# Ternary weight quantisation of the third feed-forward moved into the loop of the cross attention ahead of it

## The chip, the cores and the metric

The kernel runs on one core of one Trainium2 chip. The metric is the device time of one launch, in microseconds (us), as the median of several runs. One execution was also recorded by the hardware profiler; all rows below come from that execution.

## What is computed

The reference is a decoder of four layers on an input of 16 sequences of 128 tokens, width 256. Each layer adds an attention (or a recurrent mixer), a cross attention and a feed-forward to the residual stream `x`, each on the layer norm of `x`. The change touches two neighbours of the third layer, the cross attention and the feed-forward:

```python
def _L2_xattn_ref(q, kv, seg_id, W_kvc, W_dq, W_uq, W_qr, W_uk, W_kr, W_uv, W_o):
    kv_c = kv @ W_kvc; q_c = q @ W_dq            # latents of width 64 and 96
    # 16 heads of 128 (+ 64 rotary), scores, window mask, softmax, weighted values, @ W_o
...
def ternary_quant(w_fp32, g=64):
    w = w_fp32.astype(jnp.bfloat16)
    w_g = w.reshape(-1, g)
    scale = jnp.clip(jnp.mean(jnp.abs(w_g), axis=-1, keepdims=True), 1e-08, None)
    q = jnp.clip(jnp.round(w_g / scale), -1, 1)
    w_hat = (q * scale).reshape(w.shape)
    return w + jax.lax.stop_gradient(w_hat - w)
...
def _L2_ffn_ref(x, w_gate_up, w_proj):           # w_gate_up 2048 x 256, w_proj 256 x 1024
    gate, up = jnp.split(jnp.einsum('bsd,hd->bsh', x, ternary_quant(w_gate_up)), 2, axis=-1)
    hn = rms_norm(jax.nn.silu(gate) * up)
    return jnp.einsum('bsh,dh->bsd', hn, ternary_quant(w_proj))
...
x = x + _L2_xattn_ref(_layernorm(x), ctx_2048, itok, ...)
x = x + _L2_ffn_ref(_layernorm(x), L2_ffn_w_gate_up, L2_ffn_w_proj)
```

The quantised weights don't depend on `x`: they can be made at any time after the weights are loaded.

## The kernel before

The program is a row of twelve phases (attention, cross attention, feed-forward, four times), each written as one or two blocks in which every engine has its own instruction stream; streams meet only at semaphores, and all engines meet at the end of a block. The residual `x` stays on chip (128 partitions x 16 tiles of 256). A phase walks it in 4 groups (`GROUPS`) of 4 tiles (`TG`), 512 tokens at a time. Weights of a phase lie in one of two halves of an arena (`k.arena(n)`, tile `w` of the whole program, in the rows `all_w`); `after(sp)` is the call with which a phase lets SyncE (SP) clear the other half's semaphores and issue the loads of the next phase into the half that is free. `own` is the semaphore and count that say a phase's own weights have landed.

`phase_xattn2` (names `xattn_*` in the rows) is the third cross attention. A first block, "prep", makes products of weights: TensorE multiplies, ScalarE and VectorE copy and split them (L2792 to L2843). SP issues four small loads there (three of `l2x_qr`, one of `seg`), counted by the semaphore `small`, and the first piece of the context. ScalarE's rounding of the loaded `raw` (L2816) and VectorE's last splits (L2843) wait for `small`. The second block is a hardware loop of four passes (`Fori`), one for each group. A pass on VectorE: a mask (L2936 to L2942), the low part `ql` of the query latent (L2944), nine rotary products (L2957, L2958, L2950), then for `n` in 0 to 11 scores, maxima, normalisation, and four additions into `x` (`add`, L2988). The last, `add(3)`, waits for TensorE's last output projection (L3086); TensorE opens the next pass only after it (`step_open`). `Chain` is a helper that makes each VectorE instruction wait for the one before it. ScalarE begins a pass with `kL` (L2887). SP's stream in this block ends with `after(sp)`, behind the loads of the other context pieces.

`phase_ffn2` (names `ffn_*`) is the feed-forward; the common part is `gated_ffn`. Its first pass also prepares the weights in six chunks of 1024 columns: ScalarE casts a chunk to bf16 (L3177), VectorE's `encode` makes the 16 group scales and the codes (L3235 to L3240), GpSimd multiplies codes by scales (L3246), VectorE's `replace` forms `w + (w_hat - w)` (L3251, L3252), TensorE transposes the chunk (`turn`, L3201) and ScalarE copies it out of PSUM into `w1` or `w3` (`copy`, L3167, L3171). Chunk 0 comes ahead of the first matmul, chunks 1 to 3 ahead of the column blocks f = 2, 4, 6 of the first pass (there are 8, f = 0 to 7, each with 16 matmuls at L1179 every two), chunks 4 and 5 after them. TensorE waits for each copy before it goes on. Then come the output projection (L1188), the row sums for the RMS norm (L1196) and, in the other three groups, the same pass with no preparation.

Of the kernel before, what the change touches and what calls it, by code (L numbers as in the profile page):

```python
# [1029 lines left out]
def gated_ffn(k, w1, w2, w3, F, after, norm, parts, first, step, rms_eps=None):  # L1030
# [1680 lines left out]
def phase_xattn2(k, arena, own, after):  # L2711
# [155 lines left out]
    steps = Signal(k, "vector_steps", 5)  # L2867

    with nc.Block() as block:
        @block.sync  # L2870
        def _(sp):
# [4 lines left out]
            after(sp)  # L2876
# [52 lines left out]
        def _(dve):  # L2929
            chain = Chain(dve, steps)  # L2930
            dve.sem_inc(norm.step_open.sem, 1)
            with dve.Fori(0, GROUPS) as i:
# [57 lines left out]
                for n in range(U + 4):  # L2990
# [131 lines left out]
def phase_ffn2(k, arena, own, after):  # L3122
# [12 lines left out]
    w = k.sb("w", [P, CHUNKS, CW], BF16)  # L3135
    ratio = k.sb("ratio", [P, CW], BF16)
    code = k.sb("code", [P, 2, CW], BF16)
    scale = k.sb("scale", [P, CHUNKS, CG, 1], BF16)
    total = k.sb("total", [P, CHUNKS, CG, 1])
    inv = k.sb("inv_scale", [P, CHUNKS, CG, 1])  # L3140
    rounded = Signal(k, "rounded")
    coded = Signal(k, "coded")
    scaled = Signal(k, "codes_scaled")
    quantized = Signal(k, "quantized")
# [8 lines left out]
    def raw(c):  # L3153
        return up[:, :, c] if c < UPS else down[:, :, c - UPS]

    def rows(c):
        if c < UPS:
            return w[:, c].rearrange("p (b j n) -> p b j n", b=2, j=2)
        return w[:, c].rearrange("p (r n) -> p r n", r=KC)
# [29 lines left out]
    def turn(pe, c):  # L3189
        pe.wait_ge(*quantized(0, c + 1))  # L3190
        if c >= 2:
            pe.wait_ge(*copied(0, c - 1))
        r = rows(c)
        for h in range(KC):
            for b in range(2):
                for j in range(2):
                    if c < UPS:
                        src, at = r[:, b, j, h * P:(h + 1) * P], h * 2 * D + b * D + j * P
                    else:
                        src, at = r[:, h, (2 * b + j) * P:(2 * b + j + 1) * P], (2 * b + j) * D + h * P  # L3200
# [27 lines left out]
    def grouped(a):  # L3228
        return a.rearrange("p (g n) -> p g n", n=TGRP)

    def encode(dve, c):
        chain = chains.setdefault(0, Chain(dve, steps))
        wc = grouped(w[:, c])
        dve.wait_ge(*rounded(0, c + 1))
        chain(dve.tensor_reduce(total[:, c, :, 0], wc, AX.X, ALU.add, apply_absolute_value=True))  # L3235
        chain(dve.tensor_scalar(scale[:, c], total[:, c], 1.0 / TGRP, 1e-8, ALU.mult, ALU.max))
        chain(dve.reciprocal(inv[:, c], scale[:, c]))
        chain(dve.tensor_tensor(grouped(ratio[:, :]), wc, inv[:, c].broadcast_to([P, CG, TGRP]), ALU.mult))
        chain(dve.tensor_scalar(ratio[:, :], ratio[:, :], -1.0, 1.0, ALU.max, ALU.min))
        dve.tensor_scalar(code[:, c % 2], ratio[:, :], ROUND, ROUND, ALU.add, ALU.subtract).then_inc(coded.sem, 1)  # L3240
        dve.wait_ge(*coded(0, c + 1))

    def scale_codes(pool, c):
        qc = grouped(code[:, c % 2])
        pool.wait_ge(*coded(0, c + 1))
        pool.tensor_tensor(qc, qc, scale[:, c].broadcast_to([P, CG, TGRP]), ALU.mult).then_inc(scaled.sem, 1)  # L3246

    def replace(dve, c):
        chain = chains[0]
        dve.wait_ge(*scaled(0, c + 1))  # L3250
        chain(dve.tensor_tensor(code[:, c % 2], code[:, c % 2], w[:, c], ALU.subtract))  # L3251
# [1247 lines left out]
```

## Time and profile before

| | |
|---|---|
| median of 3 runs | 2396.2 us (2394.41 to 2402.05) |
| the profiled execution | 2391.62 us |
| its span, first to last instruction | 2389.8 us |
| TensorE busy over the span | 2103.3 us (88%) |
| VectorE / ScalarE / GpSimd busy | 66% / 52% / 13% |
| mean granted TensorE clock | 0.939 of full speed |

A busy share is an average over twelve unlike phases: it doesn't say what bounds one of them. "Idle before" an instruction is the time its engine had nothing to do just ahead of it, with what ended that time behind the arrow. Matmul ends are modelled, and a matmul's duration overlaps the next one's, so distances between starts are the better measure. PEclk is the share of TensorE's full clock (2.4 GHz) that was granted: 1.00 or 0.50, and means between them.

### The profile page before, as it was taken

To read this page: it belongs to the slowest core of one execution; us is meant where nothing else is said; L and a number is where in the kernel's file an instruction comes from. 1 tells how busy PE (TensorE), PEld (TensorE's weight loads), DVE (VectorE), ACT (ScalarE), POOL (GpSimd) and SP (SyncE) were. 2 spreads that over 40 slices of the span, in tenths; PEclk is the share of its full clock that TensorE was granted. 3 is DMA by queue.
4 is the path that set the end of the run, shared out by engine and by line. 5 is a ranking of instruction groups with operands and counts; after the bars stand their busy time and mean duration, and the time that the engine had idled before them with its cause. 6 is when DMAs were issued, how large, how long until landed. Compare 5 with 4: busy or idle time off the path is not lost. (4 is left out here: it accounts for less than half of the span.)

```text
span 2389.8 us, 46874 instructions
## 1 busy us (share of the span) xinstructions
PE 2103.3 (88%) x18948; PEld 1595.6 (67%) x18951; DVE 1576.4 (66%) x2957; ACT 1238.2 (52%) x2457; POOL 316.9 (13%) x315
## 2 busy tenths in 40 slices
PE   7979979899899898888889998958989879999996
PEld 5644437677655687566656666647756668999996
DVE  4443476667565897877858666877576676676663
ACT  3336714544466443555536446644468614666653
POOL 0010000011210000001000000011100114444342
PEclk9989989899999998999989999978989878999998
DMA  2020001100110002000010010010200025666673
GB/s 98 22 81 10 2 14 54 36 1 1 40 37 2 33 1 70 1 1 1 1 32 1 9 61 0 0 36 1 71 1 2 6 72 175 216 208 202 199 219 86
DMA packets 62649, 125.59 MB, mean 53 GB/s; under 512 B 16056, under 2 KB 45369, under 8 KB 62297
## 3 DMA queue, kind: packets, MB, share of 16 engines
q1 hardware_dynamic: 53626, 110.83, 13.8%
q0 software_dynamic: 8832, 12.06, 2.4%
q8 instruction: 138, 2.26, 0.4%
q14 instruction: 53, 0.43, 0.1%
HBM read 109.18 MB, written 15.80 MB: 52 GB/s over the span
## 5 line engine op out<-in xcount | busy, mean ns | idle before, releaser
L262 PE MATMUL ps<-ffn_xh,ffn_wh 128*128 128x256 f32 x644 | 184.0, 286 | 1.5 <-DVE ffn_xl L4283 1.5
L262 PE MATMUL ps<-ffn_xh,ffn_wl 128*128 128x256 f32 x644 | 182.3, 283 | 0.0
L262 PE MATMUL ps<-ffn_xl,ffn_wh 128*128 128x256 f32 x644 | 182.2, 283 | 0.0
L4278 DVE TENSOR_TENSOR ffn_wl<-ffn_fresh,ffn_wh 128x1792 fp32r<-128x1792 f32 x69 | 139.4, 2023 | 26.2 <-ACT ffn_wh L4158 21.1
L210 POOL TENSOR_TENSOR all_rstd<-all_mv,all_cst 128x4 f32<-128x4 f32 x41 | 9.6, 233 | 1031.8 <-DVE all_mv L193 1031.8
L1890 DVE SCALAR_TENSOR_TENSOR attn_xc<-attn_cx,all_w,attn_xc 128x512 f32<-128x512 f32 (+1 forms) x144 | 107.2, 749 | 48.0 <-ACT attn_xc L1741 44.4
L262 PEld LDWEIGHTS ps<-ffn_xh,ffn_wh 128*128 128x128 f32 x644 | 123.5, 192 | 1.7 <-DVE ffn_xl L4283 1.7
L4158 ACT ACTIVATE ffn_wh<-ffn_fresh 128x1792 fp32r<-128x1792 f32 x69 | 117.1, 1697 | 14.6 <-DMA ffn_fresh<-in_l3f_w 14.6
L262 PEld LDWEIGHTS ps<-ffn_xl,ffn_wh 128*128 128x128 f32 x644 | 123.4, 192 | 0.0
L262 PEld LDWEIGHTS ps<-ffn_xh,ffn_wl 128*128 128x128 f32 x644 | 123.4, 192 | 0.0
L2901 ACT ACTIVATE xattn_sc<-xattn_sc,xattn_mx 128x128 f32<-128x128 f32 x256 | 98.8, 391 | 17.7 <-DVE xattn_mx L2975 17.7
L4145 POOL DMA_INDIRECT x_acc<-ffn_y,ffn_row_i x46 | 79.2, 1721 | 215.0 <-ACT ffn_y L4186 212.0
L1920 DVE TENSOR_TENSOR attn_e<-attn_e,all_w 128x1024 f32<-128x1024 f32 (+1 forms) x80 | 87.2, 1124 | 16.4 <-ACT attn_e L1774 15.1
L262 PE MATMUL ps<-ffn_wh,ffn_hh 128*128 128x256 f32 x322 | 94.2, 293 | 3.9 <-issue 2.6
L1179 PE MATMUL ps<-ffn_xh,ffn_w 128*128 128x512 f32 x224 | 92.0, 411 | 6.2 <-ACT ffn_w L3167 4.5
L254 PE MATMUL ps<-all_xnT,all_w 128*128 128x512 f32 (+1 forms) x176 | 90.0, 643 | 4.1 <-ACT all_xnT L753 2.6
L262 PE MATMUL ps<-ffn_wl,ffn_hh 128*128 128x256 f32 x322 | 91.1, 283 | 0.0
L262 PE MATMUL ps<-ffn_wh,ffn_hl 128*128 128x256 f32 x322 | 91.0, 283 | 0.0
L1179 PE MATMUL ps<-ffn_xl,ffn_w 128*128 128x512 f32 x224 | 90.5, 404 | 0.0
L248 PE MATMUL ps<-all_cst 128*128 128x512 f32 x102 | 60.1, 743 | 29.6 <-ACT attn_zs L1761 10.2
L200 DVE TENSOR_SCALAR all_xn<-all_x,all_mv,all_rstd 128x256 f32<-128x256 f32 (+1 forms) x164 | 59.9, 430 | 37.5 <-POOL all_rstd L212 37.4
L4301 DVE TENSOR_TENSOR all_xnT<-ps,all_xn 128x512 f32<-128x512 f32 x92 | 57.2, 622 | 41.6 <-PE ps L262 38.7
(483 smaller groups left out, 6114.6 us busy)
## 6 DMA issues: line engine op xcount, KB each, us to landing
ffn_fresh<-in_l3f_w SPq DMA_DIRECT2D x69, 896.0 KB, 5.0
all_w<-in_ctxT SPq DMA_DIRECT2D x12, 512.0 KB, 6.2
all_w<-in_ctx SPq DMA_DIRECT2D x8, 512.0 KB, 6.5
all_x<-in_x_rows SPq DMA_DIRECT2D x4, 512.0 KB, 7.3
all_x<-x_seq SPq DMA_DIRECT2D x4, 512.0 KB, 5.4
all_w<-in_l2x_o SPq DMA_DIRECT2D x1, 2048.0 KB, 9.2
xattn_ctxT<-in_ctxT SPq DMA_DIRECT2D x4, 512.0 KB, 3.7
all_w<-in_l2f_up SPq DMA_DIRECT2D x1, 2048.0 KB, 9.1
```

The costliest lines, as they stand in the source:

```text
L200: dve.tensor_scalar(k.xn[:, t, :], k.x[:, i * TG + t, :], k.mv[:, t, 0:1], k.rstd[:, t, 0:1], ALU.subtract, ALU.mult).then_inc(self.xn_rea ...
L248: pe.matmul(k.psum[bank][:, :], k.c["ident"], k.cst[:, 0:512], start=True, stop=True)
L254: last = pe.matmul(out, w[:, c, n0:n1], k.xnT[:, c, a:b], start=start and c == 0, stop=stop and c == KC - 1)
L262: last = pe.matmul(out, a, b, start=start and n == 0, stop=stop and n == 2)
L1179: last = pe.matmul(out, w[:, c, f * P:(f + 1) * P], part[:, c, :], start=c == 0 and n == 0, stop=c == KC - 1 and n == 1)
L1890: ins = dve.scalar_tensor_tensor(out, cx[0:n, c % 2, :, j:j + P], tap, out, ALU.mult, ALU.add)
L1920: dve.tensor_tensor(e[:, d % SLOTS_E], e[:, d % SLOTS_E], gm[:, q % 2].unsqueeze(1).broadcast_to([P, HP, P]), ALU.mult).then_inc(m_ready.s ...
L2901: last = act.activation(s, s, ACT.Exp, bias=mx[:, n % nS, e, h:h + 1], scale=-1.0, accum_out=total[:, n % nS, e, h:h + 1])
L4145: pool.indirect_dma_start(acc[:, :], bass.IndirectOffsetOnAxis(ap=row_i[:, at:at + 1], axis=0), y[:, j % 2, v, :], None, compute_op=ALU.ad ...
L4158: act.activation(wh[:, j % 2, piece(q)], fresh[:, piece(q)], ACT.Copy).then_inc(high_ready.sem, 1)
L4278: dve.tensor_tensor(wl[:, j % 2, piece(q)], fresh[:, piece(q)], wh[:, j % 2, piece(q)].bitcast(F32), ALU.subtract).then_inc(low_ready.sem, 1)
L4301: dve.tensor_tensor(h[:, n % 2, 0:width], B[n % 2][:, 0:width], sa[:, n % 2, 0:width], ALU.mult).then_inc(h_ready.sem, 1)
```

## The change

- The loads of the feed-forward's weights (`after(sp)`) are issued at the head of SP's stream in the cross attention's prep block, ahead of its small loads, and no longer in the loop block.
- In each of the four passes of the cross attention ScalarE casts a quarter of the weights (1536 columns) to bf16 at the pass's head; VectorE makes the 24 group scales behind `ql`, and rounds, scales and forms the result behind `add(2)`, ahead of `add(3)`. The result is written as bf16 over the first half of the quarter's own bytes in the arena. A new semaphore pair, `tw_ready` and `tw_done`, orders the cast and the rounding; ScalarE also waits once for the loads (`k.next_own`).
- The multiplication by the scale is done by VectorE, no longer by GpSimd.
- The feed-forward's first pass has only the transposes and the copies left. The first transpose stands ahead of the layer norm's, and its copy ahead of the norm's copies. The chunks that are transposed are the same.

```diff
+    ternary = ternary_flat(k.arena(8)).rearrange("p (g n) -> p g n", g=GROUPS)
+    codes = ternary_codes(k.arena(8))
+    CW = ternary.shape[2]
+    CG = CW // TGRP
+    tw = k.sb("ternary_w", [P, CW], BF16)
+    ratio = k.sb("ternary_ratio", [P, CW], BF16)
+    group_scale = k.sb("ternary_scale", [P, CG, 1], BF16)
+    group_sum = k.sb("ternary_sum", [P, CG, 1])
+    group_inv = k.sb("ternary_inverse", [P, CG, 1])
+    tw_ready = Signal(k, "ternary_w_ready", 1)
+    tw_done = Signal(k, "ternary_w_done", 1)
...
             def _(sp):
+                after(sp)
                 qr = k.ins["l2x_qr"].rearrange("c (h r) -> c h r", h=MH)
...
                 sp.wait_ge(*ctx_used(i, 1))
                 sp.dma_start(ctxT[:, :, :], src[i + 1]).then_inc(ctx_loaded.sem, 16)
-            after(sp)
...
+            act.wait_ge(*k.next_own)
             with act.Fori(0, GROUPS) as i:
+                act.wait_ge(*tw_done(i, 1))
+                act.activation(tw[:, :], ternary[:, i, :], ACT.Copy).then_inc(tw_ready.sem, 1)
...
+            dve.sem_inc(tw_done.sem, 1)
...
+                def scale_ternary():
+                    dve.wait_ge(*tw_ready(i, 1))
+                    chain(dve.tensor_reduce(group_sum[:, :, 0], grouped(tw[:, :]), AX.X, ALU.add, apply_absolute_value=True))
+                    chain(dve.tensor_scalar(group_scale[:, :, :], group_sum[:, :, :], 1.0 / TGRP, 1e-8, ALU.mult, ALU.max))
+                    chain(dve.reciprocal(group_inv[:, :, :], group_scale[:, :, :]))
+
+                def round_ternary():
+                    wide = [P, CG, TGRP]
+                    chain(dve.tensor_tensor(grouped(ratio[:, :]), grouped(tw[:, :]), group_inv[:, :, :].broadcast_to(wide),
+                                            ALU.mult))
+                    chain(dve.tensor_scalar(ratio[:, :], ratio[:, :], -1.0, 1.0, ALU.max, ALU.min))
+                    chain(dve.tensor_scalar(ratio[:, :], ratio[:, :], ROUND, ROUND, ALU.add, ALU.subtract))
+                    chain(dve.tensor_tensor(grouped(ratio[:, :]), grouped(ratio[:, :]), group_scale[:, :, :].broadcast_to(wide),
+                                            ALU.mult))
+                    chain(dve.tensor_tensor(ratio[:, :], ratio[:, :], tw[:, :], ALU.subtract))
+                    dve.tensor_tensor(codes[:, i, 0:CW], tw[:, :], ratio[:, :], ALU.add).then_inc(tw_done.sem, 1)
+
+                scale_ternary()
...
                     if n >= 5 and n % W == 1:
+                        if n == U + 3:
+                            round_ternary()
                         add((n - 5) // W)
...
+def ternary_flat(arena):
+    return arena[:, 0:2 * TF // P * D + KC * TF]
+
+
+def ternary_codes(arena):
+    return ternary_flat(arena).bitcast(BF16).rearrange("p (g n) -> p g n", g=GROUPS)
...
     def scalar(act):
-        act.wait_ge(*own)
-        for c in range(CHUNKS):
-            act.activation(rows(c), raw(c), ACT.Copy).then_inc(rounded.sem, 1)
-            if c == 2:
-                norm.scalar(act, 0)
         copy(act, 0)
+        norm.scalar(act, 0)
 
...
     def turn(pe, c):
-        pe.wait_ge(*quantized(0, c + 1))
         if c >= 2:
             pe.wait_ge(*copied(0, c - 1))
...
     def tensor(pe):
+        turn(pe, 0)
         norm.tensor(pe, 0)
-        turn(pe, 0)
         pe.wait_ge(*copied(0, 1))
 
...
     def vector(dve):
-        norm.stats(dve, 0)
-        norm.normalize(dve, 0)
-        encode(dve, 0)
+        norm.vector(dve, 0)
         norm.split(dve, 0)
-        replace(dve, 0)
-        encode(dve, 1)
-
-    chains = {}
...
```

Where the instructions stand, first on SP at the head of the cross attention's prep block (`all_w<-in_l2f_up` and `all_w<-in_l2f_down` are the feed-forward's weights, the branches are block heads). Before:

```order
L1696 UNCONDITIONAL_BRANCH
L2767 UNCONDITIONAL_BRANCH
L2770 DMA xattn_qL<-in_l2x_qr 96x1024
L2771 DMA xattn_qL<-in_l2x_qr 96x16x32
L2772 DMA xattn_qL<-in_l2x_qr 96x16x32
L2773 DMA xattn_seg_i<-in_seg 128x16
L2774 DMA xattn_ctxT<-in_ctxT 128x2x512
```

And now:

```order
L2775 UNCONDITIONAL_BRANCH
L4431 ISA
L296 DMA all_w<-in_l2f_up 128x16x256
L296 DMA all_w<-in_l2f_down 128x2x1024
L2779 DMA xattn_qL<-in_l2x_qr 96x1024
L2780 DMA xattn_qL<-in_l2x_qr 96x16x32
L2781 DMA xattn_qL<-in_l2x_qr 96x16x32
L2782 DMA xattn_seg_i<-in_seg 128x16
L2783 DMA xattn_ctxT<-in_ctxT 128x2x512
```

A clearing of semaphores (the ISA row) and the two large loads have come ahead of the five small ones.

Then VectorE at the tail of a pass of the cross attention (`all_x<-ps,all_x` is an addition into `x`). Before:

```order
L2982 TENSOR_TENSOR xattn_sc<-xattn_sc,xattn_total 128x512 x2
L2988 ISA
L2988 TENSOR_TENSOR all_x<-ps,all_x 128x256
L2987 REGISTER_ALU
L2988 ISA
L2988 TENSOR_TENSOR all_x<-ps,all_x 128x256
L3005 MEMSET all_spare 128x1
```

And now:

```order
L3022 TENSOR_TENSOR all_x<-ps,all_x 128x256
L2969 TENSOR_TENSOR xattn_ternary_ratio<-xattn_ternary_w,xattn_ternary_inverse 128x1536
L53 REGISTER_ALU
L2971 TENSOR_SCALAR xattn_ternary_ratio<-xattn_ternary_ratio 128x1536
L53 REGISTER_ALU
L2972 TENSOR_SCALAR xattn_ternary_ratio<-xattn_ternary_ratio 128x1536
L53 REGISTER_ALU
L2973 TENSOR_TENSOR xattn_ternary_ratio<-xattn_ternary_ratio,xattn_ternary_scale 128x1536
L53 REGISTER_ALU
L2975 TENSOR_TENSOR xattn_ternary_ratio<-xattn_ternary_ratio,xattn_ternary_w 128x1536
L53 REGISTER_ALU
L2976 ISA
```

Six wide instructions now stand between the last two additions; the sixth (L2976, into `all_w`) and `add(3)` follow.

Last, TensorE at the feed-forward's head (L3201 and L3222 are `turn`, L223 the layer norm's transposes). Before:

```order
L1174 UNCONDITIONAL_BRANCH
L223 MATMUL ps<-all_cst,all_xn 128x128 x8
L3201 MATMUL ps<-all_identb,ffn_w 128x128 x8
L1179 MATMUL ps<-ffn_xh,ffn_w 128x512
L1179 MATMUL ps<-ffn_xl,ffn_w 128x512
```

And now:

```order
L1170 UNCONDITIONAL_BRANCH
L3222 MATMUL ps<-all_identb,all_w 128x128 x8
L223 MATMUL ps<-all_cst,all_xn 128x128 x8
L1175 MATMUL ps<-ffn_xh,ffn_w 128x512
L1175 MATMUL ps<-ffn_xl,ffn_w 128x512
```

The two groups of transposes have changed places, and the weights' transposes read the arena.

## Rows read from the trace of the kernel before

**Rows 1.** The page, busy time by engine: share of the span, instructions.

```profile
PE 2103.3 (88%) x18948; PEld 1595.6 (67%) x18951; DVE 1576.4 (66%) x2957; ACT 1238.2 (52%) x2457; POOL 316.9 (13%) x315
```

**Rows 2.** Windows: stretch, length, busy us by engine, PEclk, DMA share, GB/s.

```profile
1320.00:1400.00 80.00, 72.66 (x528) 54.09 (x528) 55.34 (x109) 44.68 (x165) 1.21 (x2) 1.00 0.02 7
...
1561.00:1637.00 76.00, 40.39 (x204) 33.11 (x205) 60.04 (x106) 29.24 (x41) 14.79 (x11) 0.73 0.09 28
```

**Rows 3.** Waits from 1561 to 1637: total us, times, longest.

```profile
PE ps L3201 <- DVE ffn_w L3252: 23.5, 5, 7.8
```

**Rows 4.** TensorE's timeline in the feed-forward: start, duration, [idle before].

```profile
1575.65 0.79 PE L1179 MATMUL ps<-ffn_xh,ffn_w 128*128 128x512 f32 x1 [1.11 <-ACT ffn_w L3167]
...
1582.03 0.62 PE L3201 MATMUL ps<-all_identb,ffn_w 128*128 128x128 bf16 x8
...
1583.77 0.50 PE L1179 MATMUL ps<-ffn_xh,ffn_w 128*128 128x512 f32 x1 [1.12 <-ACT ffn_w L3167]
...
1624.97 1.97 PE L223 MATMUL ps<-all_cst,all_xn 128*128 128x128 f32 x8 [3.38 <-ACT ffn_w L3171]
...
1636.24 0.40 PE L1179 MATMUL ps<-ffn_xh,ffn_w 128*128 128x512 f32 x1
...
1639.88 0.39 PE L1179 MATMUL ps<-ffn_xh,ffn_w 128*128 128x512 f32 x1
...
1661.75 0.40 PE L1179 MATMUL ps<-ffn_xh,ffn_w 128*128 128x512 f32 x1
```

**Rows 5.** Timeline of ScalarE and VectorE in the feed-forward's first pass.

```profile
1567.30 0.60 ACT L231 ACTIVATE ffn_xh<-ps 128x512 fp32r<-128x512 f32 x1 [0.26 <-PE ps L223]
...
1620.54 0.69 DVE L1147 TENSOR_TENSOR ffn_h<-ps,ffn_sa 128x512 f32<-128x512 f32 x1
```

**Rows 6.** Groups by line, 1561 to 1637: busy us, mean ns | idle before.

```profile
L3246 POOL TENSOR_TENSOR ffn_code<-ffn_code,ffn_scale 128x1024 bf16<-128x1024 bf16 x6 | 11.4, 1896 | 38.2 <-DVE ffn_code L3240 38.2
...
L3238 DVE TENSOR_TENSOR ffn_ratio<-ffn_w,ffn_inv_scale 128x1024 bf16<-128x1024 bf16 x6 | 7.3, 1224 | 0.2
L3235 DVE TENSOR_REDUCE ffn_total<-ffn_w 128x16 f32<-128x1024 bf16 x6 | 7.3, 1220 | 0.2
...
L3177 ACT ACTIVATE ffn_w<-all_w 128x1024 bf16<-128x1024 f32 x6 | 5.9, 1046 | 4.0 <-PEq L2869 4.0
...
L3252 DVE TENSOR_TENSOR ffn_w<-ffn_w,ffn_code 128x1024 bf16<-128x1024 bf16 x6 | 4.1, 691 | 0.2
...
L3239 DVE TENSOR_SCALAR ffn_ratio<-ffn_ratio 128x1024 bf16<-128x1024 bf16 x6 | 2.6, 426 | 0.2
```

**Rows 7.** The page's groups: a wider VectorE subtraction of the last phase.

```profile
L4278 DVE TENSOR_TENSOR ffn_wl<-ffn_fresh,ffn_wh 128x1792 fp32r<-128x1792 f32 x69 | 139.4, 2023 | 26.2 <-ACT ffn_wh L4158 21.1
```

**Rows 8.** Timeline of VectorE and ScalarE around the border of two passes.

```profile
1322.52 0.42 DVE L2988 TENSOR_TENSOR all_x<-ps,all_x 128x256 f32 x1 [6.82 <-PE ps L3086]
...
1330.91 0.69 DVE L2957 TENSOR_TENSOR all_w<-ps,all_cst 128x512 f32<-128x512 f32 x1 [2.68 <-PE ps L3030]
...
1325.20 0.60 ACT L2887 ACTIVATE xattn_kL<-ps 128x512 f32<-128x512 f32 x1 [5.60 <-PE ps L3016]
```

**Rows 9.** Timeline of SP, ScalarE and TensorE in the prep block.

```profile
1224.34 0.34 SPq L2770 DMA_DIRECT2D xattn_qL<-in_l2x_qr  x1
...
1228.29 0.43 SPq L2774 DMA_DIRECT2D xattn_ctxT<-in_ctxT  x1
...
1236.91 1.99 ACT L2816 ACTIVATE xattn_wh<-xattn_qL 96x1024 fp32r<-96x1024 f32 x2
...
1240.98 3.78 PE L3016 MATMUL ps<-xattn_ctxT,xattn_wkv 128*128 128x512 f32 x4 [4.39 <-DVEq L2931]
```

**Rows 10.** SP's waits, 1200 to 1650: total us, times, longest.

```profile
SPq L2766 <- DMA xattn_seg_i<-in_seg: 1.3, 1, 1.3
```

**Rows 11.** DMA issues, 1390 to 1500: KB each, us from issue to landing.

```profile
all_w<-in_l2f_up SPq DMA_DIRECT2D x1, 2048.0 KB, 9.1
all_w<-in_l2f_down SPq DMA_DIRECT2D x1, 1024.0 KB, 11.2
```

More of the change, by code:

```diff
@@ L1073, in _ @@
             norm.pool(pool, 0)
-            if "pool" in first:
-                first["pool"](pool)
             for i in range(GROUPS):
@@ L1078, in _ @@
                     norm.pool(pool, i + 1)
-                if i == 0 and "pool" in step:
-                    step["pool"](pool)
                 if rms_eps:
@@ L2866, in phase_xattn2 @@
     x_added = Signal(k, "x_added", TG)
-    steps = Signal(k, "vector_steps", 5)
+    steps = Signal(k, "vector_steps", 13)
     with nc.Block() as block:
@@ L2944, in _, with grouped @@
                 dve.tensor_tensor(ql[:, :], O[0:MQ, :], qh[:, :].bitcast(F32), ALU.subtract).then_inc(rest_ready.sem, 1)
+                def grouped(a):
+                    return a.rearrange("p (g n) -> p g n", n=TGRP)
+                def scale_ternary():
[14 more added lines that the diff above has]
+                scale_ternary()
                 def add_halves(n):
@@ L3134, in phase_ffn2, with block_at @@
     norm = Norm(k, (7, 6), (xh, xl))
[L3135 to L3144, printed above, removed]
+    codes = ternary_codes(arena)
     turned = Signal(k, "turned")
     copied = Signal(k, "copied")
-    steps = Signal(k, "prep_steps")
-    up = arena[:, 0:n_up].rearrange("p (b c j n) -> p b c j n", b=2, c=UPS, j=2)
-    down = arena[:, n_up:n_up + KC * TF].rearrange("p (r c n) -> p r c n", r=KC, c=DOWNS)
     into_w1 = w1.rearrange("p c (b n) -> p c b n", b=2)
     banks = [k.psum[b][:, :].bitcast(BF16) for b in (0, 1)]
[L3153 to L3159, printed above, removed]
+    def block_at(n):
+        width = codes.shape[2] // 2
+        return codes[:, n // width, n % width:n % width + P]
     def sync(sp):
@@ L3189, in turn @@
     def turn(pe, c):
-        pe.wait_ge(*quantized(0, c + 1))
         if c >= 2:
             pe.wait_ge(*copied(0, c - 1))
-        r = rows(c)
         for h in range(KC):
@@ L3197, in turn @@
                     if c < UPS:
[L3198 removed]
+                        src, at = block_at(b * UPS * 2 * D + (2 * c + j) * D + h * P), h * 2 * D + b * D + j * P
                     else:
[L3200 removed]
+                        src, at = block_at(n_up + h * TF + (4 * (c - UPS) + 2 * b + j) * P), (2 * b + j) * D + h * P
                     last = pe.transpose(banks[c % 2][:, at:at + P], src, k.identb[:, :])
@@ L3218, in vector @@
     def vector(dve):
-        norm.stats(dve, 0)
-        norm.normalize(dve, 0)
-        encode(dve, 0)
+        norm.vector(dve, 0)
         norm.split(dve, 0)
-        replace(dve, 0)
-        encode(dve, 1)
-    chains = {}
[L3228 to L3251, printed above, removed]
-        dve.tensor_tensor(w[:, c], w[:, c], code[:, c % 2], ALU.add).then_inc(quantized.sem, 1)
-        dve.wait_ge(*quantized(0, c + 1))
@@ L3255, in gpsimd @@
-    def gpsimd(pool):
-        for c in range(3):
-            scale_codes(pool, c)
-    def gpsimd_step(pool):
-        for c in range(3, CHUNKS):
-            scale_codes(pool, c)
-    def vector_step(dve, f):
-        if f in (1, 3, 5, 6):
-            c = {1: 1, 3: 2, 5: 3, 6: 4}[f]
-            replace(dve, c)
-            encode(dve, c + 1)
-        if f == N - 1:
-            replace(dve, CHUNKS - 1)
+    def vector_step(dve, f):
+        pass
     gated_ffn(k, w1[:, :, 0:TF], w1[:, :, TF:2 * TF], w3, TF, after, norm, (xh, xl),
-              {"sp": sync, "pool": gpsimd, "act": scalar, "dve": vector, "pe": tensor},
-              {"pool": gpsimd_step, "act": scalar_step, "dve": vector_step, "pe": tensor_step}, rms_eps=F32_EPS)
+              {"sp": sync, "act": scalar, "dve": vector, "pe": tensor},
+              {"act": scalar_step, "dve": vector_step, "pe": tensor_step}, rms_eps=F32_EPS)
@@ L4475, in build @@
                 k.start_phase(n)
+                if n + 1 < len(order):
+                    k.next_own = loads[n + 1].sem, 16 * counts[n + 1]
                 make(k, k.arena(n), (loads[n].sem, 16 * counts[n]), load_next(n + 1))
```

1 line of the change is left out of this document (removed).

## The prediction

> **What bounds the kernel now.** I read the page first: TensorE is busy 88% of the span [rows 1], so in most phases work moved between the other engines is free as long as TensorE doesn't wait for it. Then the table by stretches, which shows that this does not hold everywhere. In a pass of the third cross attention TensorE is busy 72.7 of 80 us, VectorE 55.3 and ScalarE 44.7. In the feed-forward's first pass, 1561 to 1637, TensorE is busy only 40.4 of 76 us at a mean clock of 0.73, and VectorE 60.0 [rows 2]. Third, the waits of that stretch: 23.5 us of TensorE's idle time end with VectorE's last step of a chunk (L3252) [rows 3], and 3.4 us with the copies of the last two chunks (at 1624.97) [rows 4]. So VectorE's quantisation sets the pace of this one pass. Fourth, TensorE's timeline: the first pass runs from its first L1179 at 1575.65 to the second pass's first L1179 at 1636.24, 60.6 us. The second pass, which does the same matmuls with no preparation, takes 1661.75 - 1636.24 = 25.5 us [rows 4].
>
> **What the feed-forward gains.** Six chunks of VectorE work (reduce 1.22, scales, ratio 1.22, clamp and round 0.43 each, two of 0.69) and GpSimd's 1.90 [rows 6] leave this stretch. What is then left is worked out along TensorE.
>
> Start: the input is ready when VectorE has split the norm's second half. ScalarE hands that over at 1567.30 + 0.60 = 1567.90 [rows 5]; VectorE, no longer in the middle of a chunk, needs one instruction of 0.69, L1147's length [rows 5], and TensorE starts at about 1568.65, where the trace has 1575.65: 7.0 us earlier. The first transpose and its copy now lie ahead of the norm, while TensorE would wait for the norm anyway.
>
> Length: 25.5 us for the matmuls, plus what the preparation still holds up.
> - Chunks 1, 2, 3: TensorE transposes, waits for the copy, goes on. From 1582.03 to 1583.77 that is 1.74 us [rows 4] with ScalarE free; ScalarE will now be finishing the last block's activations, so I take 1.95 each: 5.85.
> - Chunks 4 and 5: the copies stand behind ScalarE's last square. The same chain is in the trace: from the last product (L1147, 1620.54) [rows 5] to the norm's transposes at 1624.97 [rows 4] is 4.43 us, and the product starts some 0.25 after the last matmul's issue: 4.7.
> - Clock: TensorE does little between 1560 and 1568, so it will begin at 1.2 GHz. The first two column blocks took 1582.03 - 1575.65 = 6.4 us before, with the clock rising inside; at full clock sixteen matmuls take 1639.88 - 1636.24 = 3.6 [rows 4]. I take 2.2 for this, and 1.0 for a part of the output projection at the low clock after the wait for chunks 4 and 5. Bounds: 0 and 5.
>
> Sum 25.5 + 5.85 + 4.7 + 3.2 = 39.25, so the second pass starts at 1568.65 + 39.25 = 1607.9 instead of 1636.24: **28.3 us** gained. With the clock's bounds it is 26.5 to 31.5. VectorE doesn't bind again: what is left of it in the pass, 60.0 less six chunks of 4.7 to 5.1, is about 31 us for 39.
>
> **What the cross attention pays in its loop.** A quarter is 1536 columns. Prices come from the rows of 1024 columns: a plain VectorE instruction grows by (2.023 - 0.69) / (1792 - 512) = 1.04 ns a column [rows 5, 7], so ratio and reduce go from 1.22 to 1.76. The instructions that do 1024 columns in 0.69 and 0.43 grow by half and a quarter of that rate: 0.96 and 0.56 [rows 6].
> - Scales, behind `ql`: 1.76 + two small ones of about 0.2, with gaps 2.3 us. VectorE was idle there for 2.68 us, until L3030 [rows 8]. Hidden. Without that cover it would cost 2.3 a pass.
> - Round, ahead of `add(3)`: 1.76 + 0.56 + 0.56 + x + 0.96 + 0.96, and 0.04 for each of six gaps. x is the multiplication by the broadcast scale; all its operands are bf16, and VectorE has not done it in this trace. From below it is 0.96 (as L3252), from above 1.76 (as L3238, the broadcast by the inverse). I take 1.76, since L3238 has the same access to its scale. Round = 6.8 us. VectorE was idle there for 6.82 us, until the last output projection [rows 8]. So it fits with nothing to spare; `add(3)`, and behind it TensorE's next pass, may be late by what it overruns. I charge 0.1 a pass, 0.4 in all; from below 0, and 5 in all if each instruction costs 0.2 more than priced.
> - Cast on ScalarE at the pass's head: 1.05 for 1024 columns [rows 6], 1.6 at most for 1536. ScalarE was idle for 5.60 us ahead of L2887 [rows 8]; the cast can start when the round ends, near 1322.5, and is done by 1324.2, ahead of 1325.20. Hidden.
>
> For x a rule of the Trainium skill bears on the choice (VectorE: DVE Perf Modes, section "Mode 2×_1P"): two results a cycle need 16-bit operands that step by one element, which a broadcast scale does not. By that rule x is at the slow end. By the other end the round would take 6.0 us and the 0.4 would vanish; no row here has the case.
>
> **What the prep block pays.** The two loads, 3 MB, now stand ahead of the small ones in SP's queue. Issued together before, they landed 9.1 and 0.43 + 11.2 = 11.6 us after the first issue [rows 11]; the second, half as large, came 2.5 us after the first, so they were served one behind the other. Nothing waited for them then. The small loads were issued from 1224.34 on; `small` was complete at 1228.72 + 1.3 = 1230.0, and ScalarE used it at 1236.91 [rows 9, 10]: 6.9 us of slack. If the small ones are served behind 11.6 us of large ones, `small` is complete at 1236.0 plus 4 to 5.7 us (5.7 is what they took alone, start-up included). I take 1240.0. ScalarE's L2816 and, behind it, VectorE's splits, the block's end and TensorE's L3016, which waited for VectorE there [rows 9], all move by **3.1 us**. Bounds: 0 (small ones served beside the large ones) and 4.7.
>
> The Trainium skill has a rule that speaks against this part (DMA: Bandwidth & Descriptors, section "Queues, rings and completion order"): descriptors of one issuing queue are consumed in ring order on each DMA engine. The 2.5 us between the two landings agree with it. By that rule the small loads pay in full, by the lower bound they pay nothing.
>
> **Sum.** -28.3 + 0.4 + 3.1 = -24.8 us. The profiled execution took 2391.6 us, 4.6 less than the median of 2396.2; I take the difference over to the median: **2371 us**, in a profile about 2367.
>
> **Rivals.**
> - *The clock stays low.* The first pass has a gap ahead of every second column block; if these hold TensorE at 1.2 GHz, its 64 matmuls at L1179 cost up to (6.4 - 3.6) / 16 = 0.2 us more each, 13 us, of which 2 are counted: 2382. For it: clock 0.73 in the stretch [rows 2]. Against: the block after the gap of 1.12 us at 1583.77 ran at the high clock, its first matmul 0.50 long against 0.79 [rows 4]. 8%.
> - *The round overruns.* If all six instructions run at the slow rate (1.76 each), the round takes 10.8 us, 4.0 over the slot, 16 in all: 2387. For it: no slack. Against: three of its kinds were seen at the fast rates. 10%.
> - *The prep block pays nothing,* the queue serves small loads beside large ones: 2368. 15%.
> - *Slower than before.* VectorE's round becomes the loop's bound: the gain of 28.3 less 3.1 is used up when the round takes 6.3 us a pass more than its slot, 13.1 us. At GpSimd's speed for such a multiplication, 1.90 for 1024 columns [rows 6], six of 2.85 make 17 us, 10 over, 41 in all: 2396 + 16 = 2412. It would need VectorE to run the chain at GpSimd's speed; rows 6 say no. 3%.
> - *The change doesn't do what it says:* TensorE still waits for something as long as now, such as ScalarE's copies in the new order, and most of the 28 us stays: 2390 to 2399. The waits name VectorE [rows 3]. 3%.
> - The forecast itself: 61%, with 2365 to 2377.
>
> **The numbers.** 2371 is the forecast's. For 8 in 10 the range takes in the free prep block and the low clock: 2363 to 2383; it leaves out the overrunning round in full and the last two rivals. A change below 0.3% (7 us) can't be told from none; faster by more than that is everything but the last two: 94%, the same 3%, slower 3%.
>
> **What would show it.** TensorE's first L1175 after the feed-forward's head comes some 7 us after its block's first instruction, and the next pass's some 39 us later. No wait of TensorE for VectorE remains at the transposes; VectorE's idle time ahead of the last `add` of a pass falls from 6.8 to nearly 0, and two passes stay as far apart as now, to 0.5 us. In the prep block L2816's successor starts near 1240 with a DMA as the releaser. I am wrong if a cross-attention pass is over 1 us longer, if the clock in the first pass stays at 0.5, or if the feed-forward's first pass is still over 45 us.

## The result and the profile after

The changed kernel takes 2368.1 us (median of 4 runs, 2367.9 to 2370.5) where the kernel before takes 2395.3 (4 runs, 2390.9 to 2402.1): the ratio is 0.9884, 95% interval 0.9869 to 0.9899, 27 us faster. The forecast was 2371.

The profiled execution's span is 2366.1 us against 2389.8, 23.7 less. Busy times hardly move, since the same work is done elsewhere (the page's first part, answering to [rows 1]):

```profile
PE 2105.4 (89%) x18948; PEld 1596.5 (67%) x18951; DVE 1576.1 (67%) x2945; ACT 1238.8 (52%) x2455; POOL 306.0 (13%) x309
```

The table by stretches, with the columns of [rows 2]: one pass of the cross attention, and the feed-forward's first pass, which is now 46 us long.

```profile
1320.00:1400.00 80.00, 72.41 (x528) 53.67 (x526) 64.62 (x120) 46.85 (x168) 1.21 (x2) 1.00 0.02 7
1566.00:1612.00 46.00, 33.91 (x201) 28.68 (x202) 24.71 (x57) 22.58 (x35) 3.44 (x5) 0.85 0.14 47
```

VectorE went from 55.3 to 64.6 us in a pass, and from 60.0 to 24.7 in the feed-forward's first pass. TensorE's waits there (total us, times, longest) no longer name VectorE's quantisation, as [rows 3] did:

```profile
PE ps L1175 <- ACT ffn_w L3194: 3.9, 3, 1.3
PE ps L223 <- ACT ffn_w L3198: 3.6, 1, 3.6
PE ps L223 <- DVE all_xn L200: 3.1, 1, 3.1
```

**Where the time went.** The way through the program is cut at four instructions that every kernel here has: *a*, ScalarE's first copy in the prep block to TensorE's first context product; *b*, from there to the MEMSET behind the last addition of the cross attention; *c*, from there to the second pass of the feed-forward (first L1179, or its successor). What lies ahead and behind is code that no kernel here changes. All in us, from one profiled execution each:

| kernel | ahead | a | b | c (of it the first pass) | behind | span |
|---|---|---|---|---|---|---|
| before | 1225.3 | 15.70 | 319.91 | 75.35 (60.59) | 753.6 | 2389.8 |
| changed | 1228.9 | 17.27 | 319.19 | 46.58 (38.70) | 754.2 | 2366.1 |

The three changed stretches give +1.6, -0.7 and -28.8, together -27.9, which agrees with the 27.2 of the medians. The rest of the difference in the spans, +3.6 ahead and +0.6 behind, is in unchanged code. Most of the +3.6 arises in two stretches where this execution had the lower clock; here is the second in the windows, before and then after (the eighth figure is PEclk):

```profile
440.00:477.00 37.00, 28.05 (x110) 19.48 (x111) 27.56 (x62) 21.62 (x40) 5.16 (x7) 0.84 0.16 57
```

```profile
440.00:479.00 39.00, 30.39 (x119) 22.41 (x118) 27.75 (x61) 20.20 (x38) 4.09 (x6) 0.78 0.15 55
```

Over all twelve profiles of this document *ahead* runs from 1225.3 to 1232.5 us and *behind* from 747.4 to 755.4, in code that no kernel changes. So single spans differ by several us with no cause in the change; the distances a, b and c are better measures.

### The profile page after: what moved, and what is told of

It reads as the page before. It is cut to its first block and busy times, and to the rows that moved or that the text cites. A ratio compares the mean times of both kernels' runs of the same rounds, so it can differ in the third digit from the quotient of the medians.

```text
span 2366.1 us, 46893 instructions
## 1 busy us (share of the span) xinstructions
PE 2105.4 (89%) x18948; PEld 1596.5 (67%) x18951; DVE 1576.1 (67%) x2945; ACT 1238.8 (52%) x2455; POOL 306.0 (13%) x309
## 3 DMA queue, kind: packets, MB, share of 16 engines
q1 hardware_dynamic: 53626, 110.83, 13.9%
HBM read 109.18 MB, written 15.80 MB: 53 GB/s over the span
## 5 line engine op out<-in xcount | busy, mean ns | idle before, releaser
L4133 ACT ACTIVATE ffn_wh<-ffn_fresh 128x1792 fp32r<-128x1792 f32 x69 | 117.0, 1695 | 13.9 <-DMA ffn_fresh<-in_l3f_w 13.9
```

The lines of the kernel that those rows point to most:

```text
L4133: act.activation(wh[:, j % 2, piece(q)], fresh[:, piece(q)], ACT.Copy).then_inc(high_ready.sem, 1)
```

## The experiments

The theory: VectorE's chunks set the pace of the feed-forward's first pass; moved to VectorE's idle time in the cross attention they cost nothing there; and the loads moved ahead cost a little. The rivals: the first pass is slow for its clock or its copies, the loop pays somewhere, the loads don't matter. Ten kernels were run, in three sessions (e1 to e4; e5 to e8; e9 and e10). Each ratio is to the kernel before as it ran in the same session, with medians of 2397.2, 2395.5 and 2393.9 us; the changed kernel itself ran in none of them. So times of different sessions compare only to some 3 us. Stretches from one profile each:

| kernel | time, us | ratio to before (95%) | a | b | c (first pass) |
|---|---|---|---|---|---|
| e1 | 2365.4 | 0.9867 (0.9850 to 0.9884) | 15.58 | 319.91 | 45.28 (37.41) |
| e2 | 2368.9 | 0.9884 (0.9867 to 0.9900) | 17.38 | 319.02 | 46.52 (38.64) |
| e3 | 2375.5 | 0.9905 (0.9888 to 0.9921) | 17.71 | 322.07 | 46.54 (38.66) |
| e4 | 2357.7 | 0.9835 (0.9818 to 0.9851) | 17.51 | 318.95 | 37.52 (29.64) |
| e5 | 2368.2 | 0.9885 (0.9865 to 0.9905) | 15.83 | 320.07 | 48.57 (37.77) |
| e6 | 2390.8 | 0.9983 (0.9972 to 0.9993) | 17.51 | 319.25 | 74.93 (60.17) |
| e7 | 2368.6 | 0.9882 (0.9861 to 0.9903) | 17.40 | 318.95 | 46.47 (37.41) |
| e8 | 2354.7 | 0.9836 (0.9815 to 0.9858) | 15.58 | 319.84 | 37.98 (30.11) |
| e9 | 2350.0 | 0.9826 (0.9801 to 0.9852) | 15.69 | 319.98 | 34.81 (27.50) |
| e10 | 2349.1 | 0.9812 (0.9795 to 0.9828) | 15.80 | 317.20 | 34.81 (27.49) |

### Does VectorE's work set the first pass's pace? (e5)

e5 is the kernel before with the quantisation left out, so its output is not the reference's:

```diff
     def turn(pe, c):
-        pe.wait_ge(*quantized(0, c + 1))
+        pe.wait_ge(*rounded(0, c + 1))
...
         norm.stats(dve, 0)
         norm.normalize(dve, 0)
-        encode(dve, 0)
         norm.split(dve, 0)
-        replace(dve, 0)
-        encode(dve, 1)
...
     def vector_step(dve, f):
-        if f in (1, 3, 5, 6):
...
+        pass
```

GpSimd's steps are left out too; casts, transposes and copies stay.

> The kernel before with the quantisation left out of the feed-forward (VectorE's and GpSimd's parts; cast, transposes and copies stay where they are), nothing else changed. If VectorE's chunks set the pace of the first pass (theory), the pass from 1575 to 1636 gets as short as in the changed kernel or nearly so (the cast of chunk 0 still comes first, on ScalarE) and the time falls by 26 to 29 us. If TensorE's copies and transposes or the clock held it up on their own (rival), it falls by less than 20.

c fell from 75.35 to 48.57, by 26.8 us, and the first pass from 60.6 to 37.8. Nothing was moved, so the place of the loads had no part in it: VectorE's chain, with GpSimd's step in it, was the bound. The clock did not stay as it was (0.76 in the first pass before, 0.92 in e5), so some of the 22.8 us in the pass is clock that had been lost in the waits for this chain; e5 doesn't separate the two. c stays 2.0 us above the changed kernel's: the first matmul starts 10.8 us after the MEMSET, where the changed kernel has 7.9, because ScalarE's last three casts stand ahead of chunk 0's copy, and the pass behind it is 0.9 us shorter. ScalarE and TensorE in e5:

```profile
1575.28 2.94 ACT L3177 ACTIVATE ffn_w<-all_w 128x1024 bf16<-128x1024 f32 x3
1579.18 0.79 PE L1179 MATMUL ps<-ffn_xh,ffn_w 128*128 128x512 f32 x1 [3.58 <-ACT ffn_w L3167]
```

GpSimd's step cost VectorE more than the wait for its result, 0.7 us in all. GpSimd and VectorE in the kernel before:

```profile
1585.59 1.90 POOL L3246 TENSOR_TENSOR ffn_code<-ffn_code,ffn_scale 128x1024 bf16<-128x1024 bf16 x1 [6.24 <-DVE ffn_code L3240]
1586.15 1.88 DVE L1122 TENSOR_TENSOR ffn_hl<-ffn_h,ffn_hh 128x512 fp32r<-128x512 f32 x1
```

L1122 runs eight times in the first pass. The four that overlap a multiplication of GpSimd took 1.88 us each and ended 0.54 to 0.56 us after it; the other four, and all eight in e5 and in the changed kernel, took 0.68 or 0.69. That is 4.8 us of VectorE's time, and with GpSimd's multiplication out of this stretch it is gone. How much of the gain is this and how much VectorE's own instructions, no run separates.

### Does the work cost anything in the loop? (e2, e3)

e2 leaves out the scales and five of the six rounding instructions, so its weights are only cast and not quantised:

```diff
-                def scale_ternary():
+                def round_ternary():
                     dve.wait_ge(*tw_ready(i, 1))
-                    chain(dve.tensor_reduce(group_sum[:, :, 0], grouped(tw[:, :]), AX.X, ALU.add, apply_absolute_value=True))
...
-                    dve.tensor_tensor(codes[:, i, 0:CW], tw[:, :], ratio[:, :], ALU.add).then_inc(tw_done.sem, 1)
-
-                scale_ternary()
+                    dve.tensor_tensor(codes[:, i, 0:CW], tw[:, :], tw[:, :], ALU.max).then_inc(tw_done.sem, 1)
```

> The changed kernel without the scales and without five of the six rounding instructions in the cross attention's loop (the quantisation is left out; the cast and the write of the bf16 weights stay). If the loop's work lies in idle time but for about 0.1 us a pass (theory), the time falls by 0.4 us at most. If it costs elsewhere in the pass, on ScalarE's head or at the rotary products (rival), a pass gets over 0.5 us shorter and the time falls by 2 us or more.

b is 319.02 against 319.19. From one last addition to the next it is 79.44, 79.31 and 79.32 us, against 79.32, 79.31 and 79.38 in the changed kernel and 79.33, 79.34 and 79.33 in the kernel before. What e2 leaves out costs some 0.2 us in all. The cast and one wide write stay in e2; that they cost nothing either is read from the distances of the kernel before.

e3 adds an instruction to the rounding:

```diff
+                    chain(dve.tensor_tensor(spare[:, :], ratio[:, :], tw[:, :], ALU.subtract))
                     chain(dve.tensor_tensor(ratio[:, :], ratio[:, :], tw[:, :], ALU.subtract))
```

> The changed kernel with one more wide subtraction of 0.96 us in the rounding of each pass. If the idle slot at the pass's tail is exactly full (theory), each pass is 1.0 us longer and the time rises by 4.0 us. If there is slack left behind it (rival), it rises by less than 1 us.

The distances became 80.16, 80.15 and 80.15 us, 0.82 more each, and b rose by 2.9 us. The median is 6.6 us above e2's of the same session; of the total the profile finds 1.2 us in *behind* and 3.4 in *ahead* against the changed kernel's, which the edit doesn't reach; the distances carry the verdict. Of the 0.99 us added (0.96 and a gap), 0.17 found room. VectorE's timeline in e3 (start, duration) shows the last addition with no idle time ahead of it:

```profile
1329.19 0.96 DVE L2977 TENSOR_TENSOR xattn_ternary_ratio<-xattn_ternary_ratio,xattn_ternary_w 128x1536 bf16<-128x1536 bf16 x1
1330.29 0.96 DVE L2978 TENSOR_TENSOR all_w<-xattn_ternary_w,xattn_ternary_ratio 128x1536 bf16 x1
1331.16 0.42 DVE L3024 TENSOR_TENSOR all_x<-ps,all_x 128x256 f32 x1
```

So the slot is full, but for less than 0.2 us.

### What do the loads cost? (e1, e6)

e1 is the changed kernel with the large loads behind the small ones; e6 is the kernel before with them ahead.

```diff
             def _(sp):
-                after(sp)
                 qr = k.ins["l2x_qr"].rearrange("c (h r) -> c h r", h=MH)
...
                 sp.dma_start(ctxT[:, :, :], sources_xattn1(k)[1][0]).then_inc(ctx_loaded.sem, 16)
+                after(sp)
                 sp.wait_ge(*small(0, 64))
```

> The changed kernel with its two large loads issued behind the small ones in the prep block. If the large loads hold up the small ones (theory), ScalarE's rounding of the small weights no longer waits for a DMA, the prep block is 1.4 us shorter, and the time falls from 2368.1 by about 1.4 us. If the delay in the prep block had another cause (rival), the rounding starts as late as before and nothing changes.

> The kernel before with only the feed-forward's loads moved to the head of the prep block. The term of the sum by itself: 3.1 us slower by the prediction, 1.4 us by the changed kernel's trace (small loads complete 13.9 us after the first issue, ScalarE's rounding 1.4 us late). If large and small loads are served side by side (rival), no change.

a went from 17.27 back to 15.58 in e1, and from 15.70 to 17.51 in e6: the loads ahead make the prep block 1.7 to 1.8 us longer. In e6 ScalarE's rounding waits for the DMA, as in the changed kernel:

```profile
1241.11 2.00 ACT L2817 ACTIVATE xattn_wh<-xattn_qL 96x1024 fp32r<-96x1024 f32 x2 [1.64 <-DMA xattn_seg_i<-in_seg]
```

And in e1 it doesn't, while the first cast now waits for the large loads, 2.4 us in ScalarE's idle time:

```profile
1243.23 1.99 ACT L2825 ACTIVATE xattn_wh<-xattn_qL 96x1024 fp32r<-96x1024 f32 x2
1247.62 1.48 ACT L2896 ACTIVATE xattn_ternary_w<-all_w 128x1536 bf16 x1 [2.40 <-DMA all_w<-in_l2f_down]
```

Some 0.7 us come back in b, which is 319.0 to 319.3 in each profile with the loads first (e3, longer by its edit, aside) and 319.8 to 320.1 in each with them behind or in their old place (e10 aside, which changes b's clock). So the net price is 0.9 to 1.2 us. The totals can't show it: e1 is 2.7 us below the changed kernel (4.6 with each taken against the kernel before of its own session), with intervals that overlap, and e6 is *faster* than the kernel before by 0.17%, against the sign of the stretches. In e6's profile *behind* is 747.7 us against 753.6, in unchanged code; part of it is the last phase's beginning, with the higher clock in e6 (before, then e6):

```profile
1900.00:2000.00 100.00, 79.91 (x351) 62.03 (x352) 68.14 (x245) 19.37 (x28) 30.02 (x33) 0.72 0.23 77
```

```profile
1900.00:2000.00 100.00, 75.74 (x364) 57.38 (x365) 71.34 (x254) 21.31 (x30) 31.92 (x35) 0.80 0.24 84
```

Why the 12 runs of e6 were on the whole faster than those of the kernel before stays open.

e1's c is 1.3 us below the changed kernel's, in a stretch that its edit doesn't touch. That is TensorE's clock in the output projection, behind the wait of 3.62 us for the last copies that both have (windows, eighth figure; the changed kernel, then e1):

```profile
1601.00:1605.00 4.00, 4.00 (x24) 4.00 (x25) 1.29 (x2) 1.08 (x2) 0.00 (x0) 0.62 0.01 4
```

```profile
1603.00:1607.00 4.00, 4.00 (x34) 4.00 (x35) 1.29 (x2) 1.09 (x2) 0.00 (x0) 1.00 0.01 4
```

From the end of that wait to the row sums it is 6.2 us in the changed kernel, 4.8 in e1 and 7.2 in e7, for the same instructions. Why the clock fell behind this wait in some executions and not in e1's, no run here shows; a difference of 1 to 2 us in c can be this.

### What is left in the first pass? (e4, e7, e8, e9, e10)

e4 puts each transpose and copy a block earlier:

```diff
     def tensor_step(pe, f):
         if f in (2, 4, 6):
-            turn(pe, f // 2)
             pe.wait_ge(*copied(0, f // 2 + 1))
+        if f in (1, 3, 5, 6, 7):
+            turn(pe, {1: 1, 3: 2, 5: 3, 6: 4, 7: 5}[f])
         if f == N:
-            turn(pe, 4)
-            turn(pe, 5)
             pe.wait_ge(*copied(0, CHUNKS))
```

(and the same for ScalarE's `copy`).

> The changed kernel with the feed-forward's transposes and copies of chunks 1 to 5 ahead of the column blocks 1, 3, 5, 6, 7 and TensorE's waits for them one block later. What is left of the preparation is, by the theory, TensorE's waits for copies: 1.3 us at each of three and 3.6 us after the last block. They should vanish: 7 us less, 2361. If ScalarE's activations hold TensorE up as much when a copy stands ahead of them (rival), 3 us or less come back.

c fell by 9.1 us, from 46.58 to 37.52, and the total by 10.4. TensorE's waits from 1568 to 1606 in e4:

```profile
PE ps L223 <- DVE all_xn L200: 3.1, 1, 3.1
PE ps L1175 <- DVE ffn_xl L240: 1.5, 1, 1.5
PE ps L223 <- ACT ffn_w L3198: 0.5, 1, 0.5
```

The three waits for copies are gone and the last is 0.5 of 3.6: 7.0 us of waits. Of the other 2 us 1.5 are the clock of the output projection, which takes 4.8 us in e4 as in e1. Since e1 had the high clock there with the long wait in place, this part can't be put down to the edit: from e1 to e8, which differ by this edit alone, c fell by 7.3 us.

e7 is the changed kernel with six products of constants in the wait for the norm:

```diff
         turn(pe, 0)
+        idle_products(pe, k, 6, 6)
         norm.tensor(pe, 0)
```

> The changed kernel with six products of constants on TensorE, into a bank that nobody reads, between the first transposes of the feed-forward and those of the norm, in a wait of 3.1 us. If the clock is low at the pass's start only because TensorE idles there (theory), the norm's transposes and the first column blocks run at the high clock and the time falls by 2 us. If the clock comes up no sooner (rival), no change, or some 0.5 us more if the products delay the norm's transposes.

Both the theory and the rival came out: the clock was high, and the norm's transposes were pushed out. TensorE's timeline in e7 (six products stand as x12):

```profile
1569.03 5.37 PE L248 MATMUL ps<-all_cst 128*128 128x512 f32 x12
1574.24 1.04 PE L223 MATMUL ps<-all_cst,all_xn 128*128 128x128 f32 x8
1576.94 0.47 PE L1175 MATMUL ps<-ffn_xh,ffn_w 128*128 128x512 f32 x1 [1.67 <-DVE ffn_xl L240]
```

A product takes 0.9 us, so six outlast the wait, and the first matmul comes 1.2 us later. The first sixteen matmuls run at the high clock and take 3.8 us instead of 6.0, but the output projection ran 0.9 us longer at the low clock (7.2 against 6.2), and the pass is 1.3 us shorter. Nothing is left of it, and the time is the changed kernel's.

e8 is e1 and e4 together.

> The changed kernel with both the small loads first and the transposes and copies one block earlier. The two gains lie in different phases: if each holds by itself, 1.4 + 7 = 8.4 us less than the changed kernel, 2360. If one is given back in a later phase (rival), less than 7.

It keeps the 1.7 us in a and 8.6 of the 9.1 in c, against the 1.4 and 7 expected. Its time, 2354.7, is 13.4 below the changed kernel's (13.7 with each taken against the kernel before of its own session), more than the 9.6 that its stretches give; the rest stands in unchanged code and is not explained. e9 adds three products (`idle_products(pe, k, 6, 3)`), and e10 four more at the end of TensorE's stream in the prep block (`idle_products(pe, k, 7, 4)`).

> The changed kernel with small loads first, transposes and copies one block earlier, and three products of constants at the feed-forward's head (six took 5.4 us in a wait of 3.1 and pushed the norm's transposes out; three should take 2.7). If the clock is the last thing that the first pass pays for (theory), its first matmul starts as early as without products and the pass is 1.3 us shorter than with the other two edits alone: 2353.5. If three products are too little work to hold the clock (rival), the pass is as long as before.

> The same with four more products on TensorE at the end of the cross attention's prep block, where it idles for 4.4 us. If the low clock there costs the first pass of the loop (theory), the stretch from the first context product to the last addition falls from 319.9 to some 318.3 us, which is four passes of 79.33 and the way in. If the products end too late or the clock falls anyway (rival), it doesn't change or the first context product comes later.

In e9 the first matmul comes 7.3 us after the MEMSET, 0.6 earlier than in the changed kernel, since the norm's transposes run fast too, and the first pass is 27.5 us against e8's 30.1, where the second pass took 25.5 [rows 4]. That is twice the 1.3 expected; the 1.3 had been read from e7, whose output projection had given back a part. TensorE in e9:

```profile
1565.56 2.79 PE L248 MATMUL ps<-all_cst 128*128 128x512 f32 x6
1568.81 1.41 PE L223 MATMUL ps<-all_cst,all_xn 128*128 128x128 f32 x8 [0.46 <-DVE all_xn L200]
1571.72 0.47 PE L1175 MATMUL ps<-ffn_xh,ffn_w 128*128 128x512 f32 x1 [1.50 <-DVE ffn_xl L240]
```

In e10 the first context products run at full clock, 1.98 us for four where they took 3.78 [rows 9], and b is 317.20, 2.8 below e9's (1.6 expected):

```profile
1240.91 3.70 PE L248 MATMUL ps<-all_cst 128*128 128x512 f32 x8
1245.38 1.98 PE L3053 MATMUL ps<-xattn_ctxT,xattn_wkv 128*128 128x512 f32 x4 [0.77 <-DVEq L2943]
```

By time the two can't be told apart (2350.0 and 2349.1). Against the kernel before of their session they gain 43.9 and 44.7 us where the changed kernel gained 27.2: 16.7 and 17.5 more. Their stretches account for 12.6 and 15.2 of it.

## Why the prediction was right

The forecast was the likeliest case. Its main term, the feed-forward's, and the loop's held by mechanism and size; the prep block's held by mechanism and was twice too large. By the stretches the terms were off by 0.5 us (c), 1.1 (b fell by 0.7, where +0.4 was predicted) and 1.5 (a), all on the side of a larger gain; nothing cancelled.

**The feed-forward, predicted -28.3.** Measured -28.8 in c, and e5 shows the cause. Its parts can be read off TensorE's timeline after the change, answering to [rows 4]:

```profile
1573.19 0.76 PE L1175 MATMUL ps<-ffn_xh,ffn_w 128*128 128x512 f32 x1 [1.50 <-DVE ffn_xl L240]
...
1579.21 0.62 PE L3222 MATMUL ps<-all_identb,all_w 128*128 128x128 bf16 x8
1581.08 0.50 PE L1175 MATMUL ps<-ffn_xh,ffn_w 128*128 128x512 f32 x1 [1.25 <-ACT ffn_w L3194]
...
1596.23 1.07 PE L3222 MATMUL ps<-all_identb,all_w 128*128 128x128 bf16 x16
1600.92 1.09 PE L223 MATMUL ps<-all_cst,all_xn 128*128 128x128 f32 x8 [3.62 <-ACT ffn_w L3198]
...
1611.89 0.40 PE L1175 MATMUL ps<-ffn_xh,ffn_w 128*128 128x512 f32 x1
```

The start, measured from the MEMSET, is 6.9 us earlier (predicted 7.0). A transpose with its copy is 1581.08 - 1579.21 = 1.87 (1.95). The last two cost 1600.92 - 1596.23 = 4.69 (4.7). The first sixteen matmuls took 1579.21 - 1573.19 = 6.0 where 3.6 would do: 2.4 for the clock (2.2). The clock also fell behind the wait for the last copies, as forecast: it cost 1.5 us in the output projection against e1. Only 0.5 of it counts beside the second pass, whose own projection is also slower than e1's (5.7 us against 4.8), where 1.0 was forecast. The pass is 38.70 (39.25). VectorE was left with 24.7 us of work and not 31: most of the difference is the 4.8 us that L1122 had taken longer beside GpSimd, which the prediction had not seen. As VectorE didn't bind again, this changed nothing in the sum.

**The loop, predicted +0.4.** Some 0.2 by e2. VectorE's timeline at the end of a pass, with TensorE's last projection and ScalarE's cast, answering to [rows 8]:

```profile
1320.03 1.75 DVE L2969 TENSOR_TENSOR xattn_ternary_ratio<-xattn_ternary_w,xattn_ternary_inverse 128x1536 bf16<-128x1536 bf16 x1
1321.81 0.56 DVE L2971 TENSOR_SCALAR xattn_ternary_ratio<-xattn_ternary_ratio 128x1536 bf16<-128x1536 bf16 x1
...
1323.00 1.76 DVE L2973 TENSOR_TENSOR xattn_ternary_ratio<-xattn_ternary_ratio,xattn_ternary_scale 128x1536 bf16<-128x1536 bf16 x1
1324.79 0.96 DVE L2975 TENSOR_TENSOR xattn_ternary_ratio<-xattn_ternary_ratio,xattn_ternary_w 128x1536 bf16<-128x1536 bf16 x1
1325.89 0.96 DVE L2976 TENSOR_TENSOR all_w<-xattn_ternary_w,xattn_ternary_ratio 128x1536 bf16 x1
1326.93 0.42 DVE L3022 TENSOR_TENSOR all_x<-ps,all_x 128x256 f32 x1
```

```profile
1323.17 3.62 PE L3122 MATMUL ps<-xattn_wvo,xattn_zT 128*128 128x256 f32 x16
```

```profile
1326.98 1.48 ACT L2896 ACTIVATE xattn_ternary_w<-all_w 128x1536 bf16 x1 [2.96 <-DVE all_w L2976]
1329.62 0.60 ACT L2898 ACTIVATE xattn_kL<-ps 128x512 f32<-128x512 f32 x1 [1.15 <-PE ps L3052]
```

The round runs from 1320.03 to 1326.85, 6.82 us against 6.8 priced; TensorE's projection ends at 1326.79. The two meet within 0.1 us, and the last addition starts 0.14 us behind the projection's end, as in the kernel before (0.15). The unknown x, the multiplication by the broadcast scale, is 1.76, the upper bound that I chose; beside it the plain bf16 subtraction of the same width takes 0.96. This agrees with the Trainium skill's rule (VectorE: DVE Perf Modes, section "Mode 2×_1P"). The cast ends 1.15 us before ScalarE is needed.

**The prep block, predicted +3.1.** Measured +1.6 in a, and +0.9 net of what comes back in b (0.9 to 1.2 with e1 and e6). The step that was mis-sized is the delay of `small`. SP, ScalarE and TensorE after the change, answering to [rows 9], and the DMA issues (KB, us to landing), answering to [rows 11]:

```profile
1228.07 0.37 SPq L296 DMA_DIRECT2D all_w<-in_l2f_up  x1
...
1236.47 3.95 SPq L2782 DMA_DIRECT2D xattn_seg_i<-in_seg  x1
```

```profile
1242.04 2.00 ACT L2825 ACTIVATE xattn_wh<-xattn_qL 96x1024 fp32r<-96x1024 f32 x2 [1.43 <-DMA xattn_seg_i<-in_seg]
```

```profile
1246.12 3.78 PE L3052 MATMUL ps<-xattn_ctxT,xattn_wkv 128*128 128x512 f32 x4 [5.95 <-DVEq L2942]
```

```profile
all_w<-in_l2f_up SPq DMA_DIRECT2D x1, 2048.0 KB, 7.7
all_w<-in_l2f_down SPq DMA_DIRECT2D x1, 1024.0 KB, 10.5
...
xattn_qL<-in_l2x_qr SPq DMA_DIRECT2D x1, 384.0 KB, 10.0
```

The large loads were in 0.43 + 10.5 = 10.9 us after the first issue, where I took 11.6, and the small ones 3.0 us behind them, where I took 4: 1228.07 + 13.9 = 1242.0. So the two misses are 0.7 and 1.0 us of a predicted 15.7. That the small loads are held up at all, against the lower bound, e1 and e6 show; a small load that had taken at most 5.7 us alone took 10.0. This agrees with the Trainium skill's rule of ring order (DMA: Bandwidth & Descriptors, section "Queues, rings and completion order"). The prediction introduces that rule as one that speaks against this term; it speaks for it, and the prediction's next sentences use it so. Not all of the delay is behind the issue: SP took 4.3 and 4.0 us to issue the third and fourth small load, where it had taken 1.5 and 1.2, so that the fourth was issued only 8.4 us after the first large one. How much of the delay lies there, no run separates.

The 0.7 us that come back in b lie in the clock. PEclk from 1246 on before, and from 1250 on after (windows, eighth figure):

```profile
1246.00:1248.00 2.00, 2.00 (x9) 1.08 (x8) 0.00 (x0) 0.41 (x1) 0.00 (x0) 0.80 0.00 0
```

```profile
1250.00:1252.00 2.00, 2.00 (x7) 0.76 (x6) 0.00 (x0) 0.57 (x2) 0.00 (x0) 0.90 0.00 0
```

In both it was 0.50 ahead of that, so it rose some 5.8 us behind the first context product before, and some 4.3 us after. e10, with TensorE busy ahead of them, ran none of them at 1.2 GHz, and b is 2 to 3 us shorter.

**The rivals.** The clock did not stay low in the first pass: the three gaps of 1.3 us left it at 1.00; the start paid, and the output projection behind the gap of 3.6 us. The round did not overrun, but e3 shows how near that was: the next wide instruction costs 0.82 us a pass. The free prep block is refuted by e1 and e6.

## What to carry to other kernels

Work that depends on no earlier result belongs into the idle time of an engine in an earlier phase, and the idle time to look for is one long wait per pass, measured and compared with the sum of the instructions, gaps included; here 6.82 us took 6.82 us of work. Once the big cost is gone, price what stays in its place: waits for copies issued one block too late, loads in the wrong order and a low clock after a wait were worth another 15 us together, by e10's stretches. Issue large prefetches behind the small loads that the next block waits for.

## What was not expected of the hardware

- The clock of unchanged code differs between executions: 0.84 and 0.78 in one stretch, 0.72 and 0.80 in another, with *ahead* and *behind* moving by 7 to 8 us over twelve profiles. Effects of 1 us have to be read from distances inside the changed stretch, and even there the output projection was 4.8 or 6.2 us long by its clock.
- A VectorE subtraction of 128x512 in f32 took 1.88 us beside a GpSimd multiplication and 0.68 without one.
- After a wait of 5.95 us instead of 4.39 the clock rose about 1.5 us sooner behind TensorE's first product, and b was 0.7 us shorter. Why, no run here shows.
- Products of constants of 128x512 in f32 cost 0.9 us each at full clock; behind three of them in a wait of 3.1 us the next matmuls ran at 2.4 GHz, and six pushed the real work out by 1.2 us.
